# Row sums in four column tiles, a new order of the first stage and of the plan, in a latent-attention block with an FFN

## The chip, the cores and the metric

One Trainium2 chip, one core of it. The metric is the device time of one execution in microseconds. The core has a matmul engine (PE, TensorE), a vector engine (DVE, VectorE), an engine for activations and copies (ACT, ScalarE), GpSimd (POOL), and SyncE (SP), which issues the transfers.

## What is computed

Eight batches of 1024 tokens with 256 features. Each is normalised, goes through causal attention of 16 heads over a latent of 64, and through three chained linear maps with a tanh; all is added to the input.

```python
x = L0_attn_x_bld                                   # (8, 1024, 256) f32
xn = _layernorm(x, axis=-1)
# attention, H = 16, HD = 64, LD = 64
q_blhd = einsum('bld,dhk->blhk', xn, Wq)
latent_bll = einsum('bld,dc->blc', xn, Wkv_down)
k_blhd = einsum('blc,chk->blhk', latent_bll, Wk_up)
v_blhd = einsum('blc,chk->blhk', latent_bll, Wv_up)
attn = softmax(where(causal, einsum('bqhd,bkhd->bhqk', q_blhd, k_blhd) / sqrt(64), lowest))
attn_out = einsum('bqhd,hdo->bqo', einsum('bhqk,bkhd->bqhd', attn, v_blhd), Wout)
# ffn
ffn_out = tanh(((xn @ weight) @ aux_weight1) @ aux_weight2 + bias)
return x + attn_out + ffn_out
```

## The kernel before

The weights are folded once: Wq with Wk_up (wqk), Wv_up with Wout (wvo), the three FFN matrices into one (wff). Queries then meet the latent of 64 directly, which is key and value at once. Precision comes from splitting operands into a high part in the fast fp32r form and a low rest (three passes, `three_passes`, line 809); values, row sums and outputs are plain fp32.

The work is cut into units: one block of 128 queries (eight blocks a batch) with one octet of heads (two). There are 16 units in a batch, 128 in all, in segments of four whose blocks are 3, 7, 4, 0 and 5, 6, 2, 1. A unit of block i has i + 1 steps, one for each block of keys; 576 steps in all. What is done for a unit:

- MAX (line 869): scores with the queries as rows, one head and up to 512 keys at a time, into one of three banks; DVE takes the row maximum (line 1081 for the piece with the diagonal, with the causal mask added; line 1086 for a piece before it). A unit of block 4 or more has two pieces a head, and line 1092 joins the two maxima. Columns are 512, or 384, 256 or 128 at the end.
- MT (line 880): the maxima are turned into a row; ACT copies them negated, a transfer (line 1236) puts them as an extra row under q_lo, so that they enter the score matmul itself.
- ST (lines 838 and 841, two halves g a step, two banks): scores with the keys as rows; ACT takes the exponential (line 999) into one of six slots, GpSimd masks the diagonal step (line 1204) and adds the probabilities of the steps up in p_sum (line 1216).
- PV (line 855): values, one step; the two halves go to the two 64-column halves of PE's array.
- R (line 892): the sums over the partitions of p_sum (of the probabilities, for block 0) by matmuls against a matrix of ones. ACT copies them (line 1020), a transfer gathers them as [8, 128] (RG, line 1241), DVE inverts (RC, line 1098), a transfer goes to DRAM (RO, line 1246), two transfers spread them over the partitions (RB, line 1252), DVE multiplies the values by them (NM, line 1104). Three slots (Y_SLOTS).
- O (line 902, two halves O0 and O): the output product, which DVE adds (line 1113).

Beside the units run Q (two halves Q0 and Q of three passes; ACT copies q_hi, DVE subtracts q_lo, lines 1057 and 1187, two transfers double q_hi), F (the FFN product, six passes of 256 columns, with two DVE additions and a tanh), and, once a batch, normalisation (LN0 to LN4), transposes T, K and KN.

The order of all this is a plan made ahead in Python. `first_plan` is a list by hand for a first stage: loading, folding, the first batch's K and Q, and the maxima of the first AHEAD = 2 units. After a barrier comes `body_plan`, made by the class `Order`, which plays the engines' times forward by tables (PE_TIME, ACT_TIME, DVE_TIME, LANDING) and picks what PE does next: an ST if one can start, a due item if it is late (a MAX falls due at the pace of the steps that it serves, counted from the first unit not done beforehand, `max_at`), PV steps in batches of three; a change between whole-array work and the narrow kinds PV and R has its price (INTO_NARROW, OUT_OF_NARROW). Each engine's program then follows the plan in order, with waits on semaphores. p0 is the bank that Q, K, T and KN use in the body (three banks in the first stage), p1 the one for R, MT, O and F.

Of the kernel before, what the change touches and what calls it, by code (L numbers as in the profile page):

```python
# [23 lines left out]
ALU = mybir.AluOpType  # L24
ACT = mybir.ActivationFunctionType
AX = mybir.AxisListType
F32 = mybir.dt.float32
# [9 lines left out]
MAX_BANKS = 3  # L37
LOWEST = -3.0e38
# [11 lines left out]
AHEAD = 2  # L50
# [33 lines left out]
PE_TIME = {"ST": (462, 665), "PV": (846, 1070), "R": (846, 1070), "MT": (60, 330), "O0": (864, 1100),  # L84
           "O": (864, 1100), "F": (708, 920), "T": (440, 660), "K0": (693, 900), "K": (693, 900),
           "KN": (900, 1100), "Q0": (693, 900), "Q": (693, 900)}
ACT_TIME = {"ST": (510, 650), "PV": (510, 650), "MT": (255, 310), "R": (510, 650),
# [12 lines left out]
class Order:  # L100
# [170 lines left out]
    def place_max(self, ready):  # L271
# [7 lines left out]
        dve += 300 if last and k0 else 0  # L279
# [105 lines left out]
    def build(self):  # L385
        total = len(self.steps)
        while True:
# [11 lines left out]
            if self.n_pv == total and self.sum_ready() < 1e12:  # L399
                self.place_r(self.sum_ready())  # L400
                continue
            if not found:
                if n:
                    self.place_pvs(n); continue
# [36 lines left out]
def first_plan():  # L441
# [3 lines left out]
    plan += [("LN1", 0), ("LN2", 0), ("W", "constants"), ("LN3", 0)]  # L445
    plan += [("LN4", (0, k)) for k in range(2)]
    plan += [("W", "turn wq"), ("T", (0, 0, 0)), ("T", (0, 1, 0)), ("W", "fold wqk")]
    plan += [("LN4", (0, k)) for k in range(2, 4)]
    plan += [("TL", (0, 0, 0)), ("TL", (0, 1, 0))]
    for c in range(2):  # L450
        plan += [("T", (0, c, 1)), ("TL", (0, c, 1))]
    for k in range(2):
        plan += two_parts("K", (0, k)) + [("KL", (0, k))]
    plan.append(("KN", 0))
    for j in range(PAIRS):
        plan += two_parts("Q", (0, j)) + [("QL", (0, j))]
    maxima = [[("MAX", c) for c in max_chunks(u)] for u in range(AHEAD)]
    return (plan + [("W", "turn others")] + maxima[0] + [("W", "fold wvo"), ("MT", 0)] + maxima[1]
            + [("W", "fold wff"), ("MT", 1)])
# [31 lines left out]
def build(nc, x, Wq, Wkv_down, Wk_up, Wv_up, Wout, weight, aux1, aux2, bias, out):  # L491
# [6 lines left out]
    with ctx:  # L498
# [37 lines left out]
        ones = sb("ones", [P, LATENT])  # L536
        causal = sb("causal", [P, BANK])
        maxima = sb("maxima", [P, 4, OCTET])
        maxima0 = sb("maxima0", [P, 4, OCTET])
# [124 lines left out]
        def fold_on_pe(pe, what, p0_uses):  # L664
# [26 lines left out]
            if what == "constants":  # L691
                pe.wait_ge(consts_made, 7)
                pe.wait_ge(w_split, CONSTANTS)
            elif what == "turn wq":
                pe.wait_ge(wqk_loaded, 32)
                for n in range(4):
                    transposes(wq_banks[n], [wq_in[:, c, j * P:(j + 1) * P]
                                             for j in (2 * n, 2 * n + 1) for c in range(C)])
                transposes(wk_bank, [wk_in[:, j * P:(j + 1) * P] for j in range(HEADS // 2)])
            elif what == "fold wqk":  # L700

                pe.wait_ge(w_copied, 5)
                for c in range(C):
                    for g in range(2):
                        r = g * HD
                        for j in range(HEADS // 2):
                            last = nc.tensor.matmul(
                                wq_banks[2 * c + g][:, j * LATENT:(j + 1) * LATENT],
                                wqT[r:r + HD, j, c * P:(c + 1) * P], wkT[r:r + HD, j, :],
                                start=True, stop=True)  # L710
                        last.then_inc(w_full, 1)
            elif what == "turn others":
                pe.wait_ge(p0_free, p0_uses)
                pe.wait_ge(others_loaded, 96)
                transposes(ps[:, 5, :], [wv_in[:, j * P:(j + 1) * P] for j in range(HEADS // 2)])
                for bank, w in ((0, aux1_in), (1, w_in)):
                    transposes(ps[:, bank, :], [w[:, c, k * P:(k + 1) * P]
                                                for k in range(C) for c in range(C)])
            elif what == "fold wvo":
                pe.wait_ge(w_copied, 12)  # L720
                square(6, aux1T, aux2_in)
                for n, bank in enumerate((5, 0, 1)):
                    wvo_bank(bank, n)
            elif what == "fold wff":
                pe.wait_ge(w_copied, 14)
# [602 lines left out]
```

## Time and profile before

| | us |
|---|---|
| three runs, median (lowest to highest) | 2234.5 (2229.15 to 2241.65) |
| the profiled execution | 2230.46 |
| its span | 2228.7 |
| PE busy | 2125.8 |
| DVE busy | 1503.1 |
| POOL busy | 1315.1 |
| ACT busy | 1091.8 |
| granted clock of PE, mean | 0.983 |

The span is from the first to the last instruction; busy time is the union of an engine's instructions. A PE instruction's own length holds the time until its results are out, so two in a row overlap: what one costs PE is read from the distance of their starts, or from the chain of waits. The page's forty slices show the first one and a half with PE below full, and all others full. The trace's line numbers are those of the kernel before; in the changed one the same code stands a few lines further on.

### The profile page before, as it was taken

The page shows a single profiled execution, that of the slowest core. Times are in us where ns is not written, and L with a number is a line of the kernel's source. Part 1 is how long each engine was busy: PE and PEld are TensorE (multiplying, and loading weights), DVE is VectorE, ACT ScalarE, POOL GpSimd, SP SyncE. Part 2 cuts the span into 40 slices and gives each one's busy share as a digit, 9 for nine tenths or more (in the row PEclk, how much of TensorE's full clock was granted, in tenths as well). Part 3 has the DMA queues.
Part 4 walks back from the last instruction along what each step waited for, and adds up shares of the span by engine and source line. Part 5 has one row for each costly group of instructions (what it writes and reads, how often), then busy time and mean ns, then how long its engine had stood idle before and what let it go on. Part 6 is the DMA issues. An engine that isn't in the chain of part 4 may idle for free.

```text
span 2228.7 us, 31554 instructions
## 1 busy us (share of the span) xinstructions
PE 2125.8 (95%) x9400; PEld 1305.9 (59%) x9400; DVE 1503.1 (67%) x3695; ACT 1091.8 (49%) x1970; POOL 1315.1 (59%) x1163
## 2 busy tenths in 40 slices
PE   6999999999999999999999999999999999999997
PEld 4565565655666555665656556565566555566553
DVE  4667657776577676776667766767658676576662
ACT  3445554554545545455445554455455545445443
POOL 0365665656666566665566655665655666556674
PEclk8999999999999999999999999999999999999999
DMA  3011111111111111111011111111111110111111
GB/s 103 17 33 49 32 44 47 35 45 31 44 42 38 47 35 41 40 53 35 30 44 39 49 39 39 42 37 51 30 44 42 39 49 28 44 47 34 30 32 36
DMA packets 66740, 91.12 MB, mean 41 GB/s; under 512 B 12049, under 2 KB 33425, under 8 KB 66577
## 3 DMA queue, kind: packets, MB, share of 16 engines
q1 hardware_dynamic: 66576, 89.11, 14.3%
q8 instruction: 82, 1.34, 0.2%
q14 instruction: 82, 0.66, 0.1%
HBM read 45.55 MB, written 8.91 MB: 24 GB/s over the span
## 4 chain that ended last, share of the span: by engine, by line
PE 77%; DVE 10%; DMA 4%; issue 2%; ACT 2%; SPq 1%; ACTq 0%; DVEq 0%
PE ps L855 21%; PE ps L869 11%; PE ps L838 11%; PE ps L841 10%; PE ps L809 9%; PE ps L902 9%; PE ps L892 4%; DVE ps L1081 2%; DMA norm<-recips 2%; DVE maxima L1086 2%; DVE xn L1163 1%; ACT q_hi L1057 1%; DVE rows L1098 1%; DMA recips<-rows 1%; DVE norm L1104 1%
## 5 line engine op out<-in xcount | busy, mean ns | idle before, releaser
L1216 POOL TENSOR_TENSOR p_sum<-p_sum,probs 128x512 f32<-128x512 f32 x672 | 864.4, 1308 | 347.0 <-ACT probs L999 345.6
L999 ACT ACTIVATE probs<-ps 128x512 f32<-128x512 f32 x1152 | 673.8, 596 | 576.8 <-PE ps L841 544.5
L1081 DVE CUSTOM_DVE_ANT_0 ps<-ps,causal 128x256 f32<-128x256 f32 (+3 forms) x1024 | 496.4, 503 | 264.1 <-PE ps L869 255.7
L855 PE MATMUL ps<-probs,latent 128*64 128x512 f32 x2304 | 549.5, 604 | 0.0
L838 PE MATMUL ps<-q_hi,k_hilo 128*128 128x512 f32 x1152 | 511.8, 444 | 14.2 <-ACT probs L999 9.9
L869 PE MATMUL ps<-k_hilo,q_hi 128*128 128x512 f32 (+3 forms) x1536 | 480.1, 372 | 14.9 <-DVE maxima L1081 7.4
L1086 DVE TENSOR_REDUCE maxima<-ps 128x1 f32<-128x512 f32 x512 | 352.0, 687 | 197.1 <-PE ps L869 195.2
L841 PE MATMUL ps<-q_lo,k_ones 65*128 65x512 f32 x1152 | 459.3, 399 | 0.0
L869 PEld LDWEIGHTS ps<-k_hilo,q_hi 128*128 128x128 f32 x1536 | 282.1, 191 | 210.6 <-issue 106.3
L1204 POOL TENSOR_SCALAR_AFFINE_SELECT probs<-probs 128x512 f32<-128x512 f32 x256 | 166.3, 654 | 391.8 <-ACT probs L999 389.9
L1216 POOL TENSOR_TENSOR p_sum<-probs 128x512 f32<-128x512 f32 x224 | 286.7, 1294 | 152.1 <-ACT probs L999 150.6
L855 PEld LDWEIGHTS ps<-probs,latent 128*64 128x64 f32 x2304 | 152.6, 136 | 271.4 <-issue 217.1
L902 PE MATMUL ps<-wvo,norm 128*128 128x256 f32 x1024 | 265.5, 387 | 20.0 <-DVE norm L1104 17.8
L838 PEld LDWEIGHTS ps<-q_hi,k_hilo 128*128 128x128 f32 x1152 | 220.3, 191 | 104.1 <-issue 40.4
L841 PEld LDWEIGHTS ps<-q_lo,k_ones 65*128 65x128 f32 x1152 | 220.5, 191 | 27.4
L902 PEld LDWEIGHTS ps<-wvo,norm 128*128 128x128 f32 x1024 | 188.2, 191 | 68.7 <-issue 32.8
L1187 DVE TENSOR_TENSOR q_lo<-ps,q_hi 64x512 fp32r<-64x512 f32 x256 | 175.3, 685 | 22.7 <-ACT q_hi L1057 20.0
L1057 ACT ACTIVATE q_hi<-ps 64x512 fp32r<-64x512 f32 x256 | 151.6, 592 | 60.1 <-PE ps L809 52.8
L1020 ACT ACTIVATE norm<-ps 65x512 f32<-65x512 f32 x128 | 76.0, 594 | 210.0 <-PE ps L892 209.7
L1008 ACT ACTIVATE y<-ps 128x512 f32<-128x512 f32 x128 | 76.5, 597 | 161.6 <-PE ps L855 156.5
L1104 DVE TENSOR_TENSOR norm<-y,norm 128x512 f32<-128x512 f32 x128 | 110.1, 860 | 56.7 <-DMA norm<-recips 56.0
L1081 DVE DVE_READ_ACCUMULATOR2_ANT maxima<- 128x1 f32 x1024 | 140.5, 137 | 1.4
(91 smaller groups left out, 1592.2 us busy)
## 6 DMA issues: line engine op xcount, KB each, us to landing
q_hi<-q_hi SPq DMA_DIRECT2D x256, 128.0 KB, 2.3
norm<-recips SPq DMA_DIRECT2D x256, 128.0 KB, 2.8
x_in<-in_L_attn_x_bld SPq DMA_DIRECT2D x8, 1024.0 KB, 5.9
out_x<-acc SPq DMA_DIRECT2D x64, 128.0 KB, 1.7
q_lo<-rows SPq DMA_DIRECT2D x128, 4.0 KB
rows<-norm SPq DMA_DIRECT2D x128, 4.0 KB
recips<-rows SPq DMA_DIRECT2D x128, 4.0 KB
probs<-in_L_attn_Wq SPq DMA_DIRECT2D x1, 1024.0 KB, 8.1
```

The lines of the kernel that those rows point to most:

```text
L809: last = nc.tensor.matmul(dst, weights(a, c), moving(b, c), start=(c == 0 and n == 0), stop=(c == C - 1 and n == 2))
L838: nc.tensor.matmul(bank, k_hilo[par][:, blk], q_hi[seg][:, g:OCTET:2, columns(unit)], start=True, stop=False)
L841: nc.tensor.matmul(bank, k_ones[par][:, blk], q_lo[seg][:, g:OCTET:2, columns(unit)], start=False, stop=True).then_inc(st_full, 1)
L855: last = nc.tensor.matmul(y_bank[g * LATENT:(g + 1) * LATENT, :], latent[par][:, key_block(unit, s), :], probs[:, t % PT_SLOTS, g * BANK:( ...
L869: nc.tensor.matmul(max_bank[n_max % MAX_BANKS][:, 0:w], q_hi[seg % 2][:, h, columns(unit)], k_hilo[par][:, k0:k0 + w], start=True, stop=Tr ...
L902: last = nc.tensor.matmul(p1_bank[:, 0:D], norm[:, key % Y_SLOTS, j * P:(j + 1) * P], wvo[:, octet_of(key) * PAIRS + j, :], start=(j == 0) ...
L999: nc.scalar.activation(probs[:, t % PT_SLOTS, g * BANK:(g + 1) * BANK], st_bank[(2 * t + g) % ST_BANKS], ACT.Exp).then_inc(exp_done, 1)
L1057: nc.scalar.activation(q_hi[seg % 2][rows, 2 * j + g, :], p0_bank[rows, :], ACT.Copy).then_inc(p0_hi, 1)
L1081: nc.vector.tensor_tensor_reduce(bank, bank, causal[:, BANK - w:BANK], 1.0, LOWEST, ALU.add, ALU.max, maxima[:, unit % 4, h:h + 1]).then_i ...
L1086: nc.vector.tensor_reduce(maxima0[:, unit % 4, h:h + 1], bank, AX.X, ALU.max).then_inc(max_free, 1)
L1187: last = nc.vector.tensor_tensor(q_lo[seg % 2][0:LATENT, 2 * j + g, :], p0_bank[rows, :], q_hi[seg % 2][rows, 2 * j + g, :].bitcast(F32), ...
L1216: nc.gpsimd.tensor_tensor(sums, other, probs[:, slot, part], ALU.add).then_inc(pool_done, 1)
```

## The change

Six things are changed together.

1. R uses four matmuls of 32 columns of ones and 256 moving columns, each into its own quarter of the partitions, instead of two of 64 and 512. ACT copies [128, 256] instead of [65, 512], RG gathers from four partitions.
2. RB is one transfer to all 128 partitions instead of two.
3. The two maxima of a head lie side by side in `maxima`, and the join is one maximum over pairs into `joined`.
4. The first stage has another order: the small constant work on DVE is in two parts, the folding of wqk in two, the transposes of Wk stand behind the first transposes of x, fewer waits stand before "turn others", and both last folds stand in a row.
5. AHEAD is 1: the first stage makes the maxima of one unit, and the second unit's come in the body. The planner's due times for maxima are counted from there.
6. The planner's tables have other durations (R 510 instead of 846 on PE, RB 4300 instead of 3200 to landing and more), and a new rule: if nothing can start for 300 ns, it places value steps or a row sum that are ready.

```diff
-AHEAD = 2
+AHEAD = 1
-PE_TIME = {"ST": (462, 665), "PV": (846, 1070), "R": (846, 1070), ...
+PE_TIME = {"ST": (462, 665), "PV": (846, 1070), "R": (510, 730), ...
-LANDING = {"Q": 2600, "MT": 2200, "X": 6000, "RG": 2200, "RO": 2200, "RB": 3200}
+LANDING = {"Q": 2900, "MT": 2300, "X": 6000, "RG": 2600, "RO": 2200, "RB": 4300}
-INTO_NARROW, OUT_OF_NARROW = 140, 180
+INTO_NARROW, OUT_OF_NARROW = 145, 205
...
-            if self.n_pv == total and self.sum_ready() < 1e12:
-                self.place_r(self.sum_ready())
-                continue
+            if not found or min(found, key=lambda c: c[0])[0] > max(now, self.sum_ready()) + 300:
+                if n:
+                    self.place_pvs(n)
+                    continue
+                if self.sum_ready() < 1e12:
+                    self.place_r(self.sum_ready())
+                    continue
...
             elif what == "turn others":
-                pe.wait_ge(p0_free, p0_uses)
+                pe.wait_ge(p0_free, p0_uses - 2)
...
-                    for g in range(2):
-                        part = slice(g * BANK, (g + 1) * BANK)
+                    for i in range(QUADRANTS):
+                        part = slice(i * QUARTER, (i + 1) * QUARTER)
                         src = (probs[:, last_step % PT_SLOTS, part] if block_of(key) == 0
                                else p_sum[:, key % SUM_SLOTS, part])
-                        last = nc.tensor.matmul(p1_bank[g * LATENT:(g + 1) * LATENT, :], ones[:, :],
-                                                src, start=True, stop=True)
+                        last = nc.tensor.matmul(p1_bank[i * WIDTH:(i + 1) * WIDTH, 0:QUARTER],
+                                                ones[:, :], src, start=True, stop=True)
...
-                    nc.scalar.activation(norm[0:LATENT + 1, key % Y_SLOTS, :],
-                                         p1_bank[0:LATENT + 1, :],
+                    nc.scalar.activation(norm[:, key % Y_SLOTS, 0:QUARTER], p1_bank[:, 0:QUARTER],
                                          ACT.Copy).then_inc(p1_free, 1)
...
-                        nc.vector.tensor_tensor(maxima[:, unit % 4, :], maxima[:, unit % 4, :],
-                                                maxima0[:, unit % 4, :],
-                                                ALU.max).then_inc(max_joined, 1)
+                        nc.vector.tensor_reduce(joined[:, unit % 4, :], maxima[:, unit % 4, :, :],
+                                                AX.X, ALU.max).then_inc(max_joined, 1)
...
-                    for g in range(2):
-                        row = recips[slot:slot + 1, g * PAIRS:(g + 1) * PAIRS, :]
-                        sp.dma_start(norm[g * LATENT:(g + 1) * LATENT, slot, :],
-                                     row.rearrange("a j q -> a (j q)").broadcast_to([LATENT, BANK])
-                                     ).then_inc(recips_spread[slot], 16)
+                    two = recips[slot].rearrange("(g j) q -> g (j q)", g=2)
+                    sp.dma_start(norm[:, slot, :], two.unsqueeze(1).broadcast_to([2, LATENT, BANK])
+                                 ).then_inc(recips_spread[slot], 16)
```

The plan's tables move instructions on every engine. Three places follow, as PE and DVE have them in their order. In the rows, `ps<-q_hi,k_hilo` with `ps<-q_lo,k_ones` is one ST, `ps<-k_hilo,q_hi` a MAX with its columns, `probs,latent` PV (two matmuls a step), `ones` R, `wkv` half a K, `wqk` half a Q (three rows), `wff` F, `wvo,norm` half an O.

PE before, in the first batch, where the maxima of a unit are made:

```order
578 L838 MATMUL ps<-q_hi,k_hilo 128x512
579 L841 MATMUL ps<-q_lo,k_ones 128x512
580 L869 MATMUL ps<-k_hilo,q_hi 128x512
581 L838 MATMUL ps<-q_hi,k_hilo 128x512
582 L841 MATMUL ps<-q_lo,k_ones 128x512
583 L869 MATMUL ps<-k_hilo,q_hi 128x384
584 L838 MATMUL ps<-q_hi,k_hilo 128x512
585 L841 MATMUL ps<-q_lo,k_ones 128x512
```

PE in the changed kernel, about the same part of the batch. The piece begins behind the value steps of row 631 and the scores before them; the next score matmul is row 669:

```order
631 L858 MATMUL ps<-probs,latent 64x512 x6
632 L897 MATMUL ps<-p_sum,ones 32x256 x4
633 L812 MATMUL ps<-xT_hi,wqk_hi 128x512
634 L812 MATMUL ps<-xT_lo,wqk_hi 128x512
635 L812 MATMUL ps<-xT_hi,wqk_lo 128x512
636 L872 MATMUL ps<-k_hilo,q_hi 128x384
637 L872 MATMUL ps<-k_hilo,q_hi 128x512
638 L872 MATMUL ps<-k_hilo,q_hi 128x384
639 L812 MATMUL ps<-wff_hi,xT_hi 128x256
640 L812 MATMUL ps<-wff_lo,xT_hi 128x256
641 L812 MATMUL ps<-wff_hi,xT_lo 128x256
```

Before, a maxima matmul stands between two scores; now value steps, a row sum, 13 maxima matmuls (two of 512 columns, eleven of 384), three F, three Q halves and one MT stand in one stretch without a score.

PE before, where a row sum stands, behind the value steps of its unit:

```order
589 L809 MATMUL ps<-xT_hi,wkv_hi 128x512
590 L809 MATMUL ps<-xT_lo,wkv_hi 128x512
591 L809 MATMUL ps<-xT_hi,wkv_lo 128x512
592 L855 MATMUL ps<-probs,latent 64x512 x2
593 L892 MATMUL ps<-p_sum,ones 64x512 x2
```

PE in the changed kernel, two row sums of which one stands by itself:

```order
576 L872 MATMUL ps<-k_hilo,q_hi 128x256
577 L872 MATMUL ps<-k_hilo,q_hi 128x512
578 L872 MATMUL ps<-k_hilo,q_hi 128x256
579 L872 MATMUL ps<-k_hilo,q_hi 128x512
580 L872 MATMUL ps<-k_hilo,q_hi 128x384
581 L897 MATMUL ps<-probs,ones 32x256 x4
582 L872 MATMUL ps<-k_hilo,q_hi 128x512
```

A row sum no longer stands only behind value steps; of the 128, 79 do, and 49 stand between whole-array matmuls.

DVE before, at the start of the first stage:

```order
4 L772 CAST wkv_hi<-norm 128x2x64 x2
5 L773 CAST ident<-ident_f 128x64
6 L774 MEMSET ones 128x64
7 L778 TENSOR_SCALAR k_ones<-causal 1x512 x4
8 L783 TENSOR_TENSOR wkv_lo<-norm,wkv_hi 128x2x64 x2
9 L1147 RECIPROCAL ln<-ln 128x8
```

DVE in the changed kernel:

```order
6 L776 MEMSET ones 128x32
7 L1152 RECIPROCAL ln<-ln 128x8
8 L1153 TENSOR_TENSOR ln<-ln 128x8
9 L1155 TENSOR_TENSOR ln<-ln 128x8
10 L1157 TENSOR_SCALAR ln<-ln 128x8
11 L1159 TENSOR_TENSOR ln<-ln 128x8
12 L1168 TENSOR_SCALAR xn<-x_in,mean_var,ln 128x256 x4
13 L780 TENSOR_TENSOR wkv_lo<-norm,wkv_hi 128x2x64 x2
14 L786 TENSOR_SCALAR k_ones<-causal 1x512 x4
```

The six operations on wkv_lo and k_ones have moved behind the normalisation of the first half of x, and PE's first matmul no longer waits for them.

## Rows read from the trace of the kernel before

**Rows 1.** The page: its first line and the busy time of each engine.
```profile
span 2228.7 us, 31554 instructions
PE 2125.8 (95%) x9400; PEld 1305.9 (59%) x9400; DVE 1503.1 (67%) x3695; ACT 1091.8 (49%) x1970; POOL 1315.1 (59%) x1163
```

**Rows 2.** Busy us by stretch: PE, PEld, DVE, ACT, POOL, clock, DMA share, GB/s.
```profile
0.00:78.00 78.00, 51.23 (x238) 37.19 (x238) 37.84 (x100) 22.28 (x39) 1.92 (x11) 0.82 0.26 74
78.00:2205.90 2127.90, 2064.01 (x9130) 1262.63 (x9132) 1460.04 (x3587) 1067.77 (x1928) 1312.14 (x1152) 0.99 0.14 40
2205.90:2228.70 22.80, 10.52 (x34) 6.07 (x30) 5.22 (x8) 1.78 (x3) 1.06 (x1) 0.78 0.17 53
```

**Rows 3.** Timeline, PE, first stage: start us, us, instruction, idle before, releaser.
```profile
13.10 3.65 PE L687 MATMUL ps<-ident,probs 128*128 128x128 f32 x16 [13.10 <-DVE wkv_lo L783]
...
39.43 0.78 PE L809 MATMUL ps<-xT_hi,wqk_hi 128*128 128x512 f32 x1
...
50.54 0.71 PE L687 MATMUL ps<-ident,p_sum 64*128 64x64 f32 x8 [2.76 <-DVE q_lo L1187]
...
61.37 0.95 PE L869 MATMUL ps<-k_hilo,q_hi 128*128 128x512 f32 x3
...
74.22 0.27 PE L880 MATMUL ps<-ident,maxima 128*8 128x128 f32 x1
...
78.06 0.47 PE L838 MATMUL ps<-q_hi,k_hilo 128*128 128x512 f32 x1 [3.57 <-PEq L1301]
```

**Rows 4.** Loading of Wk: its issue in the timeline, and us to landing.
```profile
2.41 0.57 SPq L637 DMA_DIRECT2D p_sum<-in_L_attn_Wk_up  x1
...
p_sum<-in_L_attn_Wk_up SPq DMA_DIRECT2D x1, 256.0 KB, 8.9
```

**Rows 5.** Chain of waits, in order of time: start us, length us, what.
```profile
85.59 0.71 PE ps L809 x6
...
92.26 1.01 PE ps L855 x4
...
94.50 0.69 PE ps L809 x3
...
98.73 2.73 PE ps L855 x12
...
101.46 0.86 PE ps L892 x4
102.31 0.90 PE ps L809 x3
```

**Rows 6.** DVE groups by line and shape: busy us, mean ns, idle before.
```profile
L1187 DVE TENSOR_TENSOR q_lo<-ps,q_hi 64x512 fp32r<-64x512 f32 x256 | 175.3, 685 | 22.7 <-ACT q_hi L1057 20.0
L1081 DVE CUSTOM_DVE_ANT_0 ps<-ps,causal 128x384 f32<-128x384 f32 x256 | 142.4, 565 | 98.3 <-PE ps L869 97.6
L1098 DVE RECIPROCAL rows<-rows 8x128 f32<-8x128 f32 x128 | 120.7, 943 | 21.2 <-DMA rows<-norm 17.3
L1113 DVE TENSOR_TENSOR acc<-acc,ps 128x256 f32<-128x256 f32 x128 | 53.7, 420 | 76.3 <-PE ps L902 74.9
```

**Rows 7.** Timeline of DVE, first stage, maxima of the second unit.
```profile
66.12 0.69 DVE L1081 CUSTOM_DVE_ANT_0 ps<-ps,causal 128x512 f32<-128x512 f32 x1
...
67.33 0.69 DVE L1081 CUSTOM_DVE_ANT_0 ps<-ps,causal 128x512 f32<-128x512 f32 x1
```

**Rows 8.** Timeline of PE at a wait in the body.
```profile
479.64 0.93 PE L869 MATMUL ps<-k_hilo,q_hi 128*128 128x512 f32 x2 [1.08 <-DVE maxima L1081]
481.54 0.50 PE L809 MATMUL ps<-xT_hi,wqk_hi 128*128 128x512 f32 x1 [0.96 <-DVE q_lo L1187]
481.87 0.59 PE L809 MATMUL ps<-xT_lo,wqk_hi 128*128 128x512 f32 x1
```

**Rows 9.** Who waited for whom: total us, times, longest us.
```profile
PE ps L902 <- DVE norm L1104: 17.8, 17, 5.4
```

**Rows 10.** The two spreading transfers (line 1252): issue, and time to landing.
```profile
DMA to landing us min/median/max: 2.6/2.8/4.3
```

More of the change, by code:

```diff
@@ L278, in place_max @@
         last = h == OCTET - 1 and whole
-        dve += 300 if last and k0 else 0
+        dve += 200 if last and k0 else 0
         self.max_free.append(self.run("DVE", end, (dve, dve + (180 if whole else 130))))
@@ L444, in first_plan @@
     plan = [("LN0", (0, k)) for k in range(4)]
-    plan += [("LN1", 0), ("LN2", 0), ("W", "constants"), ("LN3", 0)]
+    plan += [("LN1", 0), ("LN2", 0), ("W", "casts"), ("LN3", 0)]
     plan += [("LN4", (0, k)) for k in range(2)]
-    plan += [("W", "turn wq"), ("T", (0, 0, 0)), ("T", (0, 1, 0)), ("W", "fold wqk")]
+    plan += [("W", "turn wq"), ("W", "residuals"), ("T", (0, 0, 0)), ("T", (0, 1, 0)),
+             ("W", "turn wk")]
     plan += [("LN4", (0, k)) for k in range(2, 4)]
[L449 to L454, printed above, removed]
+    plan += [("T", (0, c, 1)) for c in range(2)]
+    plan += [("TL", (0, c, half)) for half in range(2) for c in range(2)]
+    plan += [("W", "fold wqk 0"), *two_parts("K", (0, 0)), ("KL", (0, 0))]
+    plan += [*two_parts("K", (0, 1)), ("KL", (0, 1)), ("W", "fold wqk 1"), ("KN", 0)]
     for j in range(PAIRS):
[L456 to L459, printed above, removed]
+        plan += two_parts("Q", (0, j)) + [("QL", (0, j - 1))] * (j > 0)
+    maxima = [("MAX", c) for u in range(AHEAD) for c in max_chunks(u)]
+    return (plan + [("W", "turn others")] + maxima[:2] + [("QL", (0, PAIRS - 1))] + maxima[2:]
+            + [("W", "fold wvo"), ("W", "fold wff")] + [("MT", u) for u in range(AHEAD)])
 P0_ITEMS = ("T", "K", "KN", "Q")
@@ L740, in fold_on_act @@
                     copied(n + 1, wqT_flat[:, n * BANK:(n + 1) * BANK], wq_banks[n])
+            elif what == "turn wk":
                 copied(5, acc_flat[:, 0:512], wk_bank)
-            elif what == "fold wqk":
-                for n in range(4):
+            elif what in ("fold wqk 0", "fold wqk 1"):
+                for n in range(2 * int(what[-1]), 2 * int(what[-1]) + 2):
                     copied(6 + n, *wqk_part(wqk_hi, n), scale=HD ** -0.5)
@@ L765, in fold_on_dve @@
         def fold_on_dve(dve, what):
-            if what == "constants":
+            both = [slice(r * LATENT, (r + 1) * LATENT) for r in range(2)]
+            if what == "casts":
                 dve.wait_ge(wkv_loaded, 16)
                 dve.wait_ge(consts_made, 7)
-                both = [slice(r * LATENT, (r + 1) * LATENT) for r in range(2)]
                 for cols in both:
@@ L774, in fold_on_dve @@
                 nc.vector.memset(ones[:, :], 1.0).then_inc(w_split, 1)
+            elif what == "residuals":
+                dve.wait_ge(w_split, 2)
+                for cols in both:
+                    nc.vector.tensor_tensor(wkv_lo[:, :, cols], wkv_in,
+                                            wkv_hi[:, :, cols].bitcast(F32),
+                                            ALU.subtract).then_inc(w_split, 1)
                 for i in range(2):
```

74 lines of the change are left out of this document (36 added, 38 removed).

## The prediction

> **What bounds the kernel now.** I read the page first: TensorE is busy 2125.8 of 2228.7 us, the next engine, VectorE, 1503.1 [rows 1]. The busy time by stretch then parts the span in three: a first stage of 78 us in which PE works 51 us, often at the half clock (0.82 granted in the mean); a body of 2127.9 us with PE at work for all but 64 us of it, clock 0.99; and a tail of 22.8 us [rows 2]. So what leaves PE's row in the body leaves the time, as long as no other engine makes PE wait. The chain of waits says the same: line by line it is PE, and it gives the price of each PE step [rows 5]. One value step (L855, a third of 2.73 us less the entry) is 0.86; of the row sums L892, 0.86; three 512-column passes of L809 are 0.69, six of 256 columns 0.71, so a 512-column pass is 0.23. A change between whole-array and column-tiled work shows at both ends: 1.01 for a lone value step against 0.86 (entry 0.15), and 0.90 against 0.69 for the three passes behind a row sum (exit 0.20). A separate tiled block thus costs 0.35.
>
> **Row sums.** 128 units have one each. Two matmuls of 512 columns side by side take 0.86; four of 256 side by side should take half, 0.43. That is 128 x 0.43 = 55 us off PE. The pair in the trace shows that two column tiles do run at once: 0.86 is what one plain fp32 matmul of 512 columns needs at four passes of 0.21. Nothing shows four tiles. Bounds: 0.43, and 1.71 if they queue; I take 0.43, by the row of the pair. The Trainium skill (TensorE: Matmul & The Clock Gate, Measured speedup vs the span model) gives 2.38 times for three column tiles instead of 3; by that efficiency a row sum would be 0.54, and the sum 14 us higher. The pair in this trace loses nothing of the kind.
>
> The order changes with it. Counted in the order of PE, before has 240 tiled blocks (a row sum nearly always ends one of value steps); the changed kernel has 293, because a row sum is now also put where nothing else is ready: +53 x 0.35 = +19 us. In 79 blocks a row sum follows value steps and now changes from 64-column to 32-column tiles. No row has that change; it lies between nothing and a full exit and entry (0.35), and since the entry alone is 0.15, I take 0.10: +8 us (0 to 28). The Trainium skill (TensorEngine Tiling, Key Properties) says that a change of tiling mode drains TensorE, without a price; the entry and exit in [rows 5] agree with that.
>
> **The first stage.** PE's first matmul waits at 13.10 for the last of ten small VectorE operations [rows 3]; six of them are now behind the transposes, so it starts when Wk has landed, issued at 2.41 and 8.9 us on its way [rows 4], at 11.3: -1.8. Half of the folding matmuls stood before the first K product and half now stand behind it, in the time in which K is copied out; so Q, which starts at 39.43, starts about 8 us sooner. "Turn others" waited 2.8 us for the last two q_lo; it now waits for the second: -2.7, of which VectorE takes back 1.4, since one of these subtractions now stands among the first maxima. The second unit's 16 maxima, from 61.37 on at VectorE's pace of 0.605 each, 9.7 us, are gone from the stage, and the two folds now stand together behind the first unit's: about -9. Against that, the rest waits for PE and ACT alone. Together, -18 (-12 to -23). The body takes up these 16 passes: 16 x 0.23 = +4.
>
> **The plan, which decides it.** AHEAD falls from 2 to 1. The planner makes maxima due at the rate of the steps that they serve, counted from the first unit that is not done beforehand. Before, this lead was the 4 + 8 steps of the first two units, more than any unit's own number of steps; now it is 4, and the units of 5 to 8 steps come to their turn before their maxima are complete. The order shows it: before, scores (ST, L838) stand every one to three PE rows all through; in the changed kernel they stop in 63 places, until at least six maxima matmuls have gone by (before: 6 places). In these places PE has only work of which VectorE does more than PE: a 512-column maximum takes PE 0.23 and VectorE 0.605 (two per 1.21, [rows 7]), and PE may be three banks ahead, no more.
>
> The stretch printed above, worked through: PE has three value steps and a row sum, with entry, change and exit 3.5; three Q halves 2.1; three F 2.1; 13 maxima, two of 512 and eleven of 384 columns (0.17), 2.4; a transpose 0.1: 10.2 us. VectorE has 2 x 0.605 + 11 x 0.50 = 6.7 for the maxima (the 384 form lasts 0.565 [rows 6], shortened by overlap as the 512 form is); two q_lo at 2 x 0.685, 2.7; five additions at 0.42, 2.1; a reciprocal 0.94: 12.5. PE waits 2.3 us. Done so for all 63, PE has 577 us of work and VectorE 705; where VectorE has more, it is 128 us more in all. Each place may pass on up to three maxima to what follows (63 x 1.1 at most, some 70 less, low end 60); inside a place the two engines also wait for each other in turn, since a p0 bank comes free behind the queue of maxima, and this gives some 170, mostly 4 us for each unit of 7 or 8 steps. Queued behind each wait on PE is the unit's own transpose, behind that the row transfer, and for it wait the scores, ACT and GpSimd. I take +150 (60 to 190).
>
> **Clock.** At 478 to 481 PE idles 1.08 and 0.96 us, with shorter waits ahead, and the 512-column passes behind it last 0.59 instead of 0.40: the granted clock is at the lower level, 1.2 GHz [rows 8]. The new places hold as much idling. While PE waits for VectorE the slow clock costs nothing; what reaches into the scores does. 48 units have 6 to 8 steps or nearly so; half of them at 1 us is 24, I take +20 (0 to 110).
>
> **What goes.** The longer landing times put output products (L902) further behind their row sums: of 17.8 us waited for NM [rows 9] some 12 go. The two waits of [rows 8] recur in each of seven batches; they now fall into places that are priced already: -15. Of the body's idling and restarts, 30% of PE's work now stands in these places, where ACT isn't waited for: -25. Sum -52 (-20 to -75). One spreading transfer for two: the bytes are the same, its landing could be anything from 2.8 to the two issued in turn, 3.4 [rows 10]; hidden behind three slots, and in the tail about as before. The shorter copy of sums and the shorter row sums give the tail -2. The join is one short VectorE operation for 64 units before and after, and counts for nothing.
>
> **Sum.** 2228.7 - 55 + 19 + 8 - 18 + 4 + 150 + 20 - 52 - 2 = 2302.7, 1.8 more around the span as in the profiled run (2230.5), which lies 4 below the median of the runs: 2308.5, say 2308 us.
>
> **Rivals.** (A) The places cost little: the order has VectorE's backlog done while PE runs value steps and outputs, and the scores then come in dense groups with nothing lost. Losses of 45, no clock: 2308 - 105 - 20 = 2183. For it: GpSimd and ACT, busy 59% and 49% [rows 1], have room to catch up; against it: the sum of VectorE's own work in the 63 places. It decides where gap and clock together are under about 92 us; there the change is faster. (B) Four column tiles don't run side by side: in pairs 2363, one by one 2472. (C) The clock falls in each of the 48 longer places and stays into the scores, some 2 us each: 2308 + 80 = 2388, with 190 for the places 2428.
>
> **Chances.** Forecast 0.62 (its own range 2246 to 2370), A 0.24 (2150 to 2240), B 0.05, C 0.09. Range: 2180 to 2385, which leaves out a third of A, most of B and half of C. What a measurement of this kernel tells from no change is about 0.5%, 11 us. Faster by more: 0.22, from A; within: 0.06; slower: 0.72.
>
> **What will show it.** Row sums: four L897 matmuls in about 0.43 and the next step 0.20 later than usual; 0.86 would say pairs. First scores at about 60 us. PE's idle time in the body 150 to 200 us instead of 64, put down to VectorE's maxima and q_lo, in stretches where ACT and GpSimd are idle for 8 us and more; VectorE nearly full there. The clock row with dozens of falls. The forecast is wrong if PE idles no more than now in these places, or if value steps fill them.

## The result, and the profile after

| | before | after |
|---|---|---|
| median, us (lowest to highest) | 2236.7 (2229.15 to 2241.65) | 2567.0 (2565.44 to 2572.06) |
| ratio, with its 95% interval | | 1.148 (1.145 to 1.152) |
| span of the profiled execution | 2228.7 | 2563.7 |
| PE idle in the body | 64 | 256 |
| granted clock of PE, mean | 0.983 | 0.937 |

The changed kernel is 330 us slower. The forecast was 2308, with a range up to 2385: the sign was right, the size was not. Of 335 us more in the span, PE's own work can explain little. The page of the changed kernel, its span, its busy times, and the chain of the work that ended last, by engine and by line:

```profile
span 2563.7 us, 32433 instructions
...
PE 2277.4 (89%) x9912; PEld 1356.9 (53%) x9912; DVE 1460.8 (57%) x3695; ACT 1048.2 (41%) x1970; POOL 1305.5 (51%) x1163
...
PE 54%; DMA 22%; DVE 15%; issue 4%; SPq 2%; ACT 2%; DVEq 0%; ACTq 0%
DMA norm<-recips 15%; PE ps L858 15%; PE ps L841 10%; PE ps L844 8%; PE ps L907 7%; PE ps L872 7%; PE ps L812 5%; DMA recips<-rows 4%; DVE ps L1087 3%; DVE maxima L1092 3%; DVE q_lo L1192 2%; DVE norm L1109 2%; DMA q_lo<-rows 2%; DVE rows L1103 2%; PE ps L897 1%
```

VectorE, ACT and GpSimd are busy for no longer than before [rows 1]; PE is, by 152 us, and it idles 183 us more. What is new is in the chain: 22% of it is transfers (4% in the kernel before), 15% a single kind, `norm<-recips`. That is RB, the spreading transfer, which the prediction had hidden. The same by stretch (columns as in [rows 2]: PE, PEld, DVE, ACT, POOL, clock, DMA share, GB/s):

```profile
0.00:58.60 58.60, 39.99 (x221) 30.91 (x222) 27.67 (x75) 21.78 (x39) 1.91 (x11) 0.91 0.34 98
58.60:2540.70 2482.10, 2226.38 (x9668) 1318.64 (x9669) 1429.49 (x3614) 1026.46 (x1932) 1303.59 (x1152) 0.94 0.12 34
2540.70:2563.70 23.00, 10.98 (x24) 7.37 (x24) 3.59 (x6) 0.00 (x0) 0.00 (x0) 0.63 0.11 40
```

The first stage is shorter, 58.6 against 78.0, and the body is some 350 us longer, its clock 0.94 against 0.99. From the last score matmul to the end of the span it takes 29.2 us, where it took 24.5: in the tail nothing hides the last spreading transfer. Who waited for whom there (total us, times, longest), where [rows 9] had 17.8 us for the output product:

```profile
DVE norm L1109 <- DMA norm<-recips: 199.4, 90, 6.0
...
PE ps L907 <- DVE norm L1109: 107.6, 60, 4.6
...
DVE rows L1103 <- DMA rows<-norm: 33.7, 6, 11.2
```

One such wait, on VectorE (timeline: start us, us, instruction, idle before and releaser):

```profile
595.90 0.69 DVE L1092 TENSOR_REDUCE maxima<-ps 128x1 f32<-128x512 f32 x1
600.73 0.97 DVE L1109 TENSOR_TENSOR norm<-y,norm 128x512 f32<-128x512 f32 x1 [4.14 <-DMA norm<-recips]
601.63 1.38 DVE L1192 TENSOR_TENSOR q_lo<-ps,q_hi 64x512 fp32r<-64x512 f32 x2
608.82 0.69 DVE L1109 TENSOR_TENSOR norm<-y,norm 128x512 f32<-128x512 f32 x1 [5.81 <-DMA norm<-recips]
609.54 0.56 DVE L1087 CUSTOM_DVE_ANT_0 ps<-ps,causal 128x384 f32<-128x384 f32 x1
```

and on PE in the same stretch:

```profile
604.76 0.40 PE L872 MATMUL ps<-k_hilo,q_hi 128*128 128x512 f32 x1
610.50 2.08 PE L907 MATMUL ps<-wvo,norm 128*128 128x256 f32 x4 [5.33 <-DVE acc L1118]
```

VectorE takes its instructions in order. While it stands at NM, the maxima, q_lo and additions behind it wait too, and PE, which needs their banks, stops for 5.3 us. The chain in order of time says how long the transfers on this way take (start, length, what):

```profile
593.45 0.95 DVE rows L1103
594.42 6.46 DMA recips<-rows
600.90 7.89 DMA norm<-recips
...
630.53 1.84 DMA recips<-rows
...
668.86 7.51 DMA q_lo<-rows
```

A transfer of 4 KB, `recips<-rows` or `q_lo<-rows`, takes 6.5 to 7.5 us in these rows where a spreading transfer was issued 1.3 or 0.6 us ahead of it; the one at 630.53, with none under way, takes 1.84. From RB's issue to the start of an NM that stood waiting for it were 7.3 us (median of 90, shortest 6.8); with two transfers, in the kernel before, 3.5 (median of 41, shortest 3.3). While it runs, the DMA engines and their rate (first row: changed kernel, during the transfer; second: kernel before, during its two transfers):

```profile
594.90:599.90 5.00, 5.00 (x25) 3.11 (x25) 1.53 (x4) 3.88 (x7) 3.84 (x5) 1.00 0.14 50
```

```profile
605.40:606.30 0.90, 0.90 (x5) 0.74 (x4) 0.67 (x3) 0.41 (x1) 0.26 (x1) 1.00 0.52 159
```

0.14 of 16 engines is 2.2 engines; 0.52 is 8.3. The packets say it too: most of the single transfer's 128 packets of 2048 bytes start two at a time, a pair each 0.08 us, and all of them within 5.1 to 5.8 us, and it ends with two packets of 4 bytes; before, 128 such packets start within 1.6 us, with up to 17 under way at once, and the two transfers have 32 packets of 4 bytes. The transfer was written as [2, 64, 512], the two rows outermost, and it runs on two of the sixteen engines. The Trainium skill (DMA: Bandwidth & Descriptors, Why a DMA increments its semaphore by 16 and not by 1) states the rule: the number of engines is the largest up to 16 that divides the slowest dimension, other than 1, of both sides. Of 2 and 128 that is 2. The trace agrees, and the prediction hadn't weighed it.

### The profile page after: what moved, and what is told of

The parts are those of the page before. It is cut to its first block, busy times and chain, and to the rows that moved or that the text cites. A ratio compares the mean times of both kernels' runs of the same rounds, so it can differ in the third digit from the quotient of the medians.

```text
span 2563.7 us, 32433 instructions
## 1 busy us (share of the span) xinstructions
PE 2277.4 (89%) x9912; PEld 1356.9 (53%) x9912; DVE 1460.8 (57%) x3695; ACT 1048.2 (41%) x1970; POOL 1305.5 (51%) x1163
## 4 chain that ended last, share of the span: by engine, by line
PE 54%; DMA 22%; DVE 15%; issue 4%; SPq 2%; ACT 2%; DVEq 0%; ACTq 0%
DMA norm<-recips 15%; PE ps L858 15%; PE ps L841 10%; PE ps L844 8%; PE ps L907 7%; PE ps L872 7%; PE ps L812 5%; DMA recips<-rows 4%; DVE ps L1087 3%; DVE maxima L1092 3%; DVE q_lo L1192 2%; DVE norm L1109 2%; DMA q_lo<-rows 2%; DVE rows L1103 2%; PE ps L897 1%
## 5 line engine op out<-in xcount | busy, mean ns | idle before, releaser
L1006 ACT ACTIVATE probs<-ps 128x512 f32<-128x512 f32 x1152 | 652.4, 596 | 713.4 <-PE ps L844 700.2
L841 PE MATMUL ps<-q_hi,k_hilo 128*128 128x512 f32 x1152 | 546.8, 475 | 34.4 <-DMA q_lo<-rows 26.7
L872 PE MATMUL ps<-k_hilo,q_hi 128*128 128x512 f32 (+3 forms) x1536 | 504.4, 398 | 62.5 <-DVE maxima L1087 34.5
L844 PE MATMUL ps<-q_lo,k_ones 65*128 65x512 f32 x1152 | 481.0, 418 | 0.0
L907 PE MATMUL ps<-wvo,norm 128*128 128x256 f32 x1024 | 305.1, 435 | 128.8 <-DVE norm L1109 107.6
L907 PEld LDWEIGHTS ps<-wvo,norm 128*128 128x128 f32 x1024 | 212.8, 216 | 205.0 <-issue 127.7
L844 PEld LDWEIGHTS ps<-q_lo,k_ones 65*128 65x128 f32 x1152 | 235.6, 205 | 27.8
L1109 DVE TENSOR_TENSOR norm<-y,norm 128x512 f32<-128x512 f32 x128 | 126.8, 991 | 199.8 <-DMA norm<-recips 199.4
L1118 DVE TENSOR_TENSOR acc<-acc,ps 128x256 f32<-128x256 f32 x128 | 53.7, 420 | 226.9 <-PE ps L907 226.0
L1103 DVE RECIPROCAL rows<-rows 8x128 f32<-8x128 f32 x128 | 120.7, 943 | 37.5 <-DMA rows<-norm 33.7
```

The source lines that it names most:

```text
L841: nc.tensor.matmul(bank, k_hilo[par][:, blk], q_hi[seg][:, g:OCTET:2, columns(unit)], start=True, stop=False)
L844: nc.tensor.matmul(bank, k_ones[par][:, blk], q_lo[seg][:, g:OCTET:2, columns(unit)], start=False, stop=True).then_inc(st_full, 1)
L872: nc.tensor.matmul(max_bank[n_max % MAX_BANKS][:, 0:w], q_hi[seg % 2][:, h, columns(unit)], k_hilo[par][:, k0:k0 + w], start=True, stop=Tr ...
L907: last = nc.tensor.matmul(p1_bank[:, 0:D], norm[:, key % Y_SLOTS, j * P:(j + 1) * P], wvo[:, octet_of(key) * PAIRS + j, :], start=(j == 0) ...
L1006: nc.scalar.activation(probs[:, t % PT_SLOTS, g * BANK:(g + 1) * BANK], st_bank[(2 * t + g) % ST_BANKS], ACT.Exp).then_inc(exp_done, 1)
L1103: nc.vector.reciprocal(row_sums[:, slot, :], row_sums[:, slot, :]).then_inc(recip_done, 1)
```

## The experiments

Theory T: two losses. The single transfer is slow and VectorE's queue stands behind it; and the 63 places without scores cost what the forecast named. Rivals: R1, the places alone, dearer than forecast; R2, the slow clock by itself; R3, four column tiles don't run together. All ratios are to the kernel before, on the same chip.

### Two transfers again, all else as changed

```diff
-                    two = recips[slot].rearrange("(g j) q -> g (j q)", g=2)
-                    sp.dma_start(norm[:, slot, :], two.unsqueeze(1).broadcast_to([2, LATENT, BANK])
-                                 ).then_inc(recips_spread[slot], 16)
+                    for g in range(2):
+                        row = recips[slot:slot + 1, g * PAIRS:(g + 1) * PAIRS, :]
+                        sp.dma_start(norm[g * LATENT:(g + 1) * LATENT, slot, :], ...
```

> The changed kernel with the spreading made by two transfers again, all else as it is, the plan too. Theory T (the single transfer, 7.3 us to its consumer instead of 3.5, is what the forecast missed): the time falls from 2567 to about the forecast, 2290 to 2330, waits of PE for the normalised values from 108 us to under 30, low-clock time from 312 us to under 150. Theory P (the plan with AHEAD = 1 costs all of it, the transfer is hidden): it stays over 2500.

Measured: 2381.2 us, 1.065 (1.061 to 1.068); 186 us less than the changed kernel. DVE's wait for the transfer fell from 199.4 to 15.0 us, PE's for NM from 107.6 to 23.1:

```profile
PE ps L907 <- DVE norm L1109: 23.1, 22, 3.6
...
DVE norm L1109 <- DMA norm<-recips: 15.0, 14, 3.3
```

R1 alone falls: 186 of the 330 us hang on how this transfer is written. R2, the slow clock by itself, falls with it. Nothing in the edit touches the clock, yet the body's time at 1.2 GHz fell from 297 to 161 us. In 269 and 151 us of these PE was busy; half of that difference, some 59 of the 186 us, is an estimate of the clock's part.

### One transfer, its rows not outermost

```diff
-                    two = recips[slot].rearrange("(g j) q -> g (j q)", g=2)
-                    ... two.unsqueeze(1).broadcast_to([2, LATENT, BANK])
+                    row = recips[slot:slot + 1, 0:PAIRS, :]
+                    ... row.rearrange("a j q -> a (j q)").broadcast_to([P, BANK])
```

> The changed kernel with one transfer of the same bytes whose outermost dimension is 128 instead of 2: it spreads one row of 512 over all partitions, so half of the heads are multiplied by the wrong inverse; nothing else is left out. If the single transfer is slow because its outermost dimension of 2 leaves it to 2 of the 16 DMA engines, issue to consumer falls from 7.3 to 3.0 to 3.5 us and the time is that of the two transfers within 10 us. If it is slow because one transfer of 256 KB is, it stays at 7 us and the time at 2567.

Measured: 2380.8 us, 1.064 (1.061 to 1.067), and 3.2 to 3.9 us from issue to a waiting NM (7 cases). It writes the same number of bytes as in the changed kernel, and is one transfer too; its outermost dimension is 128 instead of 2, and it reads one row of 2 KB instead of two. The run with two transfers reads both rows and takes the same time. The pages' rows of packets, of this kernel and of the changed one:

```profile
DMA packets 64950, 91.17 MB, mean 38 GB/s; under 512 B 10256, under 2 KB 31632, under 8 KB 64784
```

```profile
DMA packets 63158, 91.16 MB, mean 36 GB/s; under 512 B 8464, under 2 KB 29840, under 8 KB 62992
```

1792 more packets under 512 bytes are 14 more for each of the 128 transfers, as with one closing packet of 4 bytes from each of 16 engines instead of 2. So it isn't that there is one transfer, but its shape.

### AHEAD 2, with one transfer and with two

```diff
-AHEAD = 1
+AHEAD = 2
```

> The changed kernel with AHEAD = 2: the maxima of two units ahead, the plan made accordingly, the single transfer kept. Theory P: 2170 to 2200. Theory T: the slow transfer still costs most of its share, over 2350. Both: in between, 2230 to 2350.

> The changed kernel with AHEAD = 2 and two transfers. What is left is the shorter row sum, the first stage and the corrected table. By the sum of the prediction without the terms of the places (150), their clock (20) and the shorter first stage (9): about 2150; with row sums at 0.57 instead of 0.53 as measured, 2155. Both theories give 2140 to 2185.

Measured: with the single transfer 2455.2 us, 1.096 (1.093 to 1.100); with two, 2168.3 us, 0.968 (0.965 to 0.971). The second differs from the changed kernel in two edits and is 68 us faster than the kernel before, where the changed kernel is 330 slower. With two transfers AHEAD 1 thus costs 213 us (2381 against 2168); the single transfer costs 287 in this plan, 186 in the other.

### The single transfer alone, in the kernel before

```diff
-                    for g in range(2): ...
+                    two = recips[slot].rearrange("(g j) q -> g (j q)", g=2)
+                    ... two.unsqueeze(1).broadcast_to([2, LATENT, BANK])
```

> The kernel before with the single spreading transfer alone. With two transfers for one, the AHEAD = 2 kernel lost 287 us to it (2455 against 2168). If that is the transfer in itself, the kernel before loses as much here: 2480 to 2540. If it needs the changed plan, which puts output products closer, it loses far less: 2240 to 2350.

Measured: 2645.2 us, 1.183 (1.181 to 1.185): +410 us by this one edit.

```profile
DVE norm L1104 <- DMA norm<-recips: 425.6, 115, 8.8
...
PE ps L902 <- DVE norm L1104: 206.4, 66, 9.4
```

115 of the 128 multiplications stood waiting. Here the planner counts on a landing of 3200 ns, in the changed kernel on 4300: the earlier NM is placed, the longer VectorE stands. That this is why the cost is 410 and not 287 is argued; the next runs change the landings alone.

### The planner told of the slow transfer

```diff
-LANDING = {..., "RB": 4300}
+LANDING = {..., "RB": 7600}
```

> AHEAD = 2 and the single transfer, but the planner is told that it lands after 7600 ns instead of 4300. If the loss comes from NM standing too early in the order of VectorE, which waits in it while maxima stand behind it, most of the 287 us returns: 2170 to 2230. If it comes from the length of the chain itself (three slots, other transfers held up behind it on the queue), it stays over 2350.

Measured: 2309.6 us, 1.033 (1.030 to 1.036). Half of the 287 us came back, by the order alone. PE's wait for NM was 20.3 us now, but VectorE's for the gathered sums, `DVE rows L1103 <- DMA rows<-norm`, had grown to 101.5 us in 36 waits, from 17.1 in 8 with two transfers. So other small transfers, held up behind the slow one, were the candidate for the rest; the three slots for the outputs were the other. A run raised all the landings:

```diff
-LANDING = {"Q": 2900, "MT": 2300, "X": 6000, "RG": 2600, "RO": 2200, "RB": 7600}
+LANDING = {"Q": 5400, "MT": 4800, "X": 6000, "RG": 5100, "RO": 4700, "RB": 7600}
```

> The changed kernel with AHEAD 2 and the single spreading transfer, planned at 7600 as in the run that gave 2310 us, and now the landings of the other small transfers raised too (Q 2900 to 5400, MT 2300 to 4800, RG 2600 to 5100, RO 2200 to 4700), since a slow spreading transfer in flight holds them up. With two transfers the same kernel took 2168. If the remaining 142 us are engines that wait for transfers held up, which the plan didn't know of: 2180 to 2240. If they are the longer way from row sums to the output product with three slots for it, which a plan can't take away and which longer planned landings stretch further: 2300 or more.

Measured: 2157.0 us, 0.963 (0.959 to 0.967), below the expected 2180 to 2240: against the 2168 with two transfers nothing is left of the transfer's cost, though an NM that waits for it still starts 7.2 us after its issue (median of 22). Two transfers in this same order were not run.

```profile
DVE norm L1109 <- DMA norm<-recips: 28.4, 22, 7.6
...
PE ps L907 <- DVE norm L1109: 26.3, 20, 8.6
...
DVE rows L1103 <- DMA rows<-norm: 16.5, 4, 8.0
```

The slots are not the cause. What costs is an order made for transfers that land sooner than they do.

### AHEAD 1 with its maxima due earlier

```diff
-        self.max_at = list(itertools.accumulate([c[3] / (OCTET * P) for c in self.maxima], initial=0))
+        self.max_at = list(itertools.accumulate([c[3] / (OCTET * P) for c in self.maxima], initial=-8))
```

with two transfers, as in the next one, where it is -4.

> Two transfers, AHEAD = 1, and the due times of all maxima eight steps earlier, which gives them the lead of AHEAD = 2 in the body; the first stage stays the short one (first scores at 61 us instead of 70). If the 213 us of AHEAD = 1 come from the lead alone, 2160 to 2180; the 8 places without scores and with six maxima in its order (63 with AHEAD = 1) speak for it. If it is the missing second unit at the start, it stays near 2380.

> Two spreading transfers, AHEAD 1, maxima due 4 steps earlier than in the changed kernel (0 steps earlier gave 2381 us, 8 steps 2158). In the order 7 places without scores have six maxima or more, against 63 and 8. If the loss of AHEAD 1 is these places, 2155 to 2175. If it is a lead of too few steps in itself, it falls half way: about 2270.

Measured: 2158.2 us, 0.965 (0.963 to 0.967), at 8 steps; 2168.2 us, 0.969 (0.965 to 0.973), at 4. At none it was 2381. The expectation of the second run says 7 places of six maxima or more; the order in fact has 32 (the changed kernel 63, the run at 8 steps has 8). They are short, though: 30 of 6 or 7 maxima and two of 10, against 50 of 11 to 18 in the changed order. So the loss isn't proportional to the lead, nor to the number of places: it comes with the long ones. PE's body from 65 us on, at none and at 8 steps:

```profile
65.00:2353.90 2288.90, 2153.81 (x9618) 1276.86 (x9618) 1426.33 (x3611) 1019.77 (x1922) 1303.44 (x1146) 0.96 0.13 37
```

```profile
65.00:2134.20 2069.20, 2029.73 (x9638) 1239.01 (x9637) 1429.42 (x3605) 1033.12 (x1926) 1314.44 (x1149) 0.99 0.15 41
```

220 us apart: 96 are idle time (135.1 against 39.5; of the 135.1, 105.1 lie inside the 63 places). The other 124 are PE busy with the same matmuls. About 53 of these are the clock, which was at 1.2 GHz for 161 us of the body against 44; PE was busy in 151 and 44 of them, and half of that difference is lost. Another 12 are 34 more tiled blocks at 0.35 [rows 5]. The rest, some 60, is by difference; waiting that the rows count as busy, as in the stretch that follows, is the likely cause.

The prediction worked one stretch through. Here it is in the run with two transfers, AHEAD 1 (PE, then VectorE):

```profile
312.17 2.79 PE L858 MATMUL ps<-probs,latent 128*64 128x512 f32 x12
314.90 0.64 PE L897 MATMUL ps<-p_sum,ones 128*32 128x256 f32 x8
...
316.27 0.74 PE L872 MATMUL ps<-k_hilo,q_hi 128*128 128x384 f32 x3
...
317.56 1.28 PE L872 MATMUL ps<-k_hilo,q_hi 128*128 128x512 f32 x3
...
320.56 0.50 PE L812 MATMUL ps<-xT_hi,wqk_hi 128*128 128x512 f32 x1 [0.75 <-DVE q_lo L1192]
...
325.07 1.24 PE L872 MATMUL ps<-k_hilo,q_hi 128*128 128x384 f32 x3
326.56 0.50 PE L841 MATMUL ps<-q_hi,k_hilo 128*128 128x512 f32 x1 [0.25 <-DMA q_lo<-rows]
```

```profile
316.64 0.56 DVE L1087 CUSTOM_DVE_ANT_0 ps<-ps,causal 128x384 f32<-128x384 f32 x1 [4.41 <-PE ps L872]
```

```profile
312.17:326.56 14.39, 12.33 (x63) 7.08 (x62) 9.81 (x28) 5.05 (x10) 1.99 (x2) 1.00 0.20 48
```

14.4 us for 10.2 of PE's work: 4.2 lost, not 2.3. Of the 12.5 us forecast for VectorE 9.8 lie within the place; three of the 13 maxima, part of the second q_lo and two additions pass on to what follows. VectorE first stands idle for 4.4, as PE does value steps and a row sum, which give it nothing; only then does it do its 9.8 us, nearly without a gap, and PE waits for it three matmuls at a time. The first three maxima, which nothing holds up, are shown as 0.74; the later threes are shown as 1.28 and 1.24, with starts up to 0.53 apart instead of 0.17 to 0.23: most of the difference is waiting, and the busy row counts it.

### Row sums as before

AHEAD 2, two transfers, but R by two matmuls of 64 columns of ones and 512 moving ones, and its old durations in the planner.

```diff
-                    for i in range(QUADRANTS):
-                        part = slice(i * QUARTER, (i + 1) * QUARTER)
+                    for g in range(2):
+                        part = slice(g * BANK, (g + 1) * BANK)
...
-ones = sb("ones", [P, WIDTH])
+ones = sb("ones", [P, LATENT])
```

> AHEAD = 2, two transfers, and the row sums as before: two matmuls of 64 columns and 512, the old copy, with 855 ns in the plan's table. Measured in the trace a row sum behind value steps now costs 0.57 us against 0.86; 128 x 0.29 = 37 us, less the separate blocks. So 2168 + 25 to 40 = 2193 to 2208. Under 2180 the row sums bring nothing.

Measured: 2204.3 us, 0.986 (0.984 to 0.987). The four tiles are worth 36 us (2204 against 2168; 39 by the two ratios, as the runs are from two chips). Behind value steps a row sum costs 0.57, where [rows 5] has 0.86 (chain of the changed kernel):

```profile
658.36 2.73 PE ps L858 x12
661.09 0.57 PE ps L897 x8
```

R3 falls: one after the other, four would need 1.71.

### Landings once more

The same AHEAD 1 kernel (8 steps, two transfers) with RB planned at 3700, nearer to what two transfers need; then the changed kernel with the long landings and nothing else; then AHEAD 1, 8 steps, the single transfer, the long landings.

> The changed kernel with two spreading transfers and the maxima due 8 steps earlier (2158 us), and now the planner's landing time for the spreading transfer at 3700 instead of 4300, which is nearer to what two transfers take (3.5 us from issue to the start of the multiplication). If the product after the row sums now stands later than it need, a few us come off: 2150 to 2158. If a landing planned too early makes VectorE hold its queue again, 2165 or more. Neither theory of the large loss hangs on it.

> The changed kernel (AHEAD 1, single spreading transfer, 2567 us) with nothing changed but the planned landings of the small transfers (5400, 4800, 5100, 4700 and 7600 for Q, MT, RG, RO, RB). With two transfers the same kernel took 2381. In the order 68 places without scores have six maxima or more (63 in the changed kernel). If the 186 us of the slow transfer are the mismatch of plan and landing alone: 2340 to 2400, the loss of the places being left. If the places and the slow transfer feed each other: 2450 or more.

> AHEAD 1 with maxima due 8 steps earlier, the single spreading transfer and the long planned landings: two transfers and the short landings gave 2158, AHEAD 2 with the long ones 2157. If the first stage, 8 us shorter at AHEAD 1, adds to the long landings: 2145 to 2155. The order has 22 places without scores, one with ten maxima and the others with six; if these cost, 2160 to 2180.

Measured, in this order: 2167.9 us, 0.968 (0.964 to 0.973); 2502.6 us, 1.122 (1.116 to 1.127); 2149.8 us, 0.962 (0.960 to 0.964). The first: VectorE waited 45.6 us for the transfer, in 30 waits, against 16.4 in 10 with 4300, so the shorter figure looks too short already; the two times, 2168 and 2158, have ratios whose intervals touch. The second: with AHEAD 1 and late maxima the long landings give back 64 of the 186 us. VectorE still waited 102.3 us for the spreading transfer, in 37 waits, and the new order has 68 places, 54 of them with 12 maxima or more. So in the changed kernel longer landings alone don't give the transfer's cost back; that this is because the order made for slow transfers has longer places is likely, and not shown. The third has the shortest time here, 85 us (3.8%) below the kernel before, though its interval overlaps those of the runs at 2157 and 2158. It is the changed kernel but for due times and landings.

## Why the prediction was wrong

**One spreading transfer.** This step failed. The prediction said that its landing "could be anything from 2.8 to the two issued in turn, 3.4 [rows 10]; hidden behind three slots", and counted it at nothing. [rows 10] is a bound for transfers of the old shape; bytes were compared, the shape was not. It took 7.3 us, not 3.4, and cost 186 us. "Hidden behind three slots" was wrong as well: the slots hide it from PE only if VectorE isn't made to stand for it, and VectorE's order was fixed for 4.3. The prediction asked that question for the maxima and not here. With this term at nothing the sum is to be held against 2381, and is 73 us short of it.

**The plan's places.** Right in mechanism, short in size: +150, and +20 for the clock. AHEAD 1 as a whole measured +213 (2381 against 2168), and these are wholly recovered by earlier due times. The sums of VectorE's and PE's work in a place were compared (12.5 against 10.2), as if both began together. They don't: VectorE is idle first. Less than half of the loss is seen as idle time (135 us in the body with two transfers, 105 of them inside the places, where the forecast had 150 to 200 in the body), the rest as longer busy time.

**What goes.** Forecast -52: 12 for output products, 15 for the waits of [rows 8], 25 for idling that was to fall into the places. The 12 did not come off: PE's wait for NM, 17.8 us before, was 22.0 at AHEAD 2 and 23.1 at AHEAD 1, with two transfers. The other 40 belong to the places. With them the sum has 150 + 20 + 4 - 9 + 12 (34 of the 53 blocks) - 40 = 137 for AHEAD 1, where 213 were measured, and that makes up the 73. The rest of the sum comes to 2171 against 2168, but partly by luck, with the 12 wrong and some 24 found elsewhere.

**Clock.** +20 forecast. With two transfers the body spent 161 us at the low level, and lost some 53 us more to it than the run without long places; in the changed kernel it spent 297 us there, in 61 falls, against 38 in eight before. Rival C, the clock falling in the longer places and staying into the scores (2388 to 2428), was thus part of what happened, beside the forecast and not in its place. Its time, 2388, comes near 2381 by luck: it puts 80 on top of the forecast's 20 by clock alone, where the clock took 53 and the waits in the places the rest.

**Row sums.** Forecast 0.43, plus 0.10 for the change of tiles; measured 0.57 behind value steps. Rival B is refuted. The term -55 + 19 + 8 = -28 goes with 293 blocks. In the run with the old row sums the order had 249 blocks, with four tiles 259; 36 us and ten blocks at 0.35 make 0.31 a row sum, so on average 0.55 instead of 0.86, the change of tiles included. The trace of the changed kernel parts the row sum from the change. From its start to that of the whole-array matmul behind it are 0.57 us, behind value steps (78 cases) and behind whole-array matmuls (26) alike, where it was 0.96 before (120): 0.39 less with the same exit, so 0.47 for a row sum by itself instead of 0.86. From the last value matmul's start to the row sum's it went from 0.42 to 0.52: the change of tiles is the 0.10 that was taken without a row. The prediction's other sum, by the Trainium skill (TensorE: Matmul & The Clock Gate, Measured speedup vs the span model), had 0.54 without that change. The trace's 0.47 lies between it and the 0.43 of the row of the pair.

**First stage.** Right. First matmul at 11.37 (forecast 11.3), first scores at 58.6 (about 60; 61.5 in the run with two transfers, whose first stage is the same). The timeline of PE, for [rows 3]:

```profile
11.37 3.53 PE L689 MATMUL ps<-ident,probs 128*128 128x128 f32 x16 [11.37 <-DMA p_sum<-in_L_attn_Wk_up]
...
31.07 0.50 PE L812 MATMUL ps<-xT_hi,wqk_hi 128*128 128x512 f32 x1 [0.40 <-DVE wqk_lo L793]
...
54.69 0.28 PE L885 MATMUL ps<-ident,maxima 128*8 128x128 f32 x1
58.62 0.47 PE L841 MATMUL ps<-q_hi,k_hilo 128*128 128x512 f32 x1 [3.66 <-PEq L1304]
```

Q starts 8.4 us sooner (forecast about 8). Between AHEAD 1 and 2 the first scores lie 8 us apart with two transfers (61.5 and 69.6) and 14 with one (58.6 and 72.9), forecast about 9.

**Tail.** Forecast -2. It became 4.7 us longer with the single transfer, and 6 us shorter (18.2) with two at AHEAD 1. "In the tail about as before" falls with the first step.

**Rival A**, little loss in the places, 2183: false for the changed order, and true as soon as the places are short (2168 with 32 of them).

**The account.** The kernel before 2236. Row sums -36, the first stage at AHEAD 2 about -8 (first scores at 69.6 instead of 78.1; -5 by the other runs at AHEAD 2), and the rest of the new plan, by difference, some -24: 2168. AHEAD 1 with late maxima +213: 2381. The single transfer +186: 2567. What in the new plan gives the 24 was not tried apart; the idle time of PE in the body is 14 us less. Nor is the waiting hidden in busy rows, some 60 of the 213, measured by itself.

## What to carry to other kernels

Before a transfer is counted as "the same bytes", look at its outermost dimension on both sides: 2 there made it take 7.3 us where 128 took about 3.5. In a kernel whose order is made ahead, a wait's price depends on what is queued behind it: the same slow transfer cost 410, 287, 186 or nothing, by the order that it met, and what the plan took its landing and that of its neighbours to be decided over much of that. And where two engines feed each other in a stretch, add the time in which one has no input yet; their sums of work alone give too little.

## What the runs showed of the hardware

- One transfer of 256 KB with an outermost dimension of 2: DMA share 0.14 and 50 GB/s while it runs, 7.3 us to a waiting instruction; as two transfers of half the size, 0.52, 159 GB/s and 3.5 us; as one with 128 outermost, 3.2 to 3.9 us.
- Transfers of 4 KB issued while it is under way took up to 7.5 us, against 1.84 without it, though the DMA share while it ran was 0.14, 2.2 of 16 engines.
- Four fp32 matmuls in 32-column tiles, 256 columns each, add 0.57 us behind 64-column tiles, of which 0.10 is the change of tiles.
- A matmul's busy time can hold waiting: three passes that are shown as 0.74 us when nothing holds them stood as 1.24 to 1.28 in the row, without idle time ahead of them.
